# A recurrent mixer kernel on one core: the scan put last in each step of TensorE's program

## The reference, cut to what matters

```python
proj = xn @ in_proj_w.T                      # gate 8192, x 8192, B and C 8 x 128 each, dt 128
xBC  = silu(causal_conv4(xBC))               # per channel, 4 taps
# per head (128 heads of 64 channels, 8 groups of 16 heads), chunks of 128 tokens:
scores = (C @ B.T) * exp(cs[l] - cs[s]) * (s <= l)
y = scores @ (x * dt) + state terms + x * D
yg = y * silu(gate);  per group: yg * rsqrt(mean(yg**2) + eps) * norm_w
out = x_in + (yg @ out_proj_w.T) * silu(experts(xn))
```

## Time and profile before

| | |
|---|---|
| median of 3 runs | 1605.9 us (1604.34 to 1606.1) |
| profiled execution | 1605.15 us, span 1603.2 us |
| TensorE, matmul | 1588.8 us busy, 99% |
| TensorE, weight load | 1267.1 us, 79% |
| VectorE | 1409.1 us, 88% |
| ScalarE | 1196.3 us, 75% |
| GpSimd | 961.7 us, 60% |
| granted TensorE clock | 0.999 |
| a stream load, issue to landing | 2.7 us (median of 387) |
| a load of exponents | 4.3 us (median of 128) |
| one transpose, mean | 272 ns |

### The profile page before, as it was taken

One profiled execution on the slowest core, in us unless ns is written; L12 is line 12 of the kernel. 1 busy time (PEld: TensorE's weight loads), 2 busy tenths in 40 slices (PEclk: granted clock), 3 DMA queues, 4 the chain that ended last, 5 costly groups with the idle time before them and its releaser, 6 DMA issues.

```text
span 1603.2 us, 28456 instructions
## 1 busy us (share of the span) xinstructions
PE 1588.8 (99%) x8478; PEld 1267.1 (79%) x8478; DVE 1409.1 (88%) x1654; ACT 1196.3 (75%) x2305; POOL 961.7 (60%) x596
## 2 busy tenths in 40 slices
PE   9999999999999999999999999999999999999998
PEld 6888777887778777887778777887778777877776
DVE  7727899889999899889998899889998899889987
ACT  4525878777787878777787878777787878778772
POOL 6523456655666556655666556655666666656563
PEclk9999999999999999999999999999999999999999
DMA  5234344334443344344443334334443334334442
GB/s 187 75 136 148 126 137 169 118 131 143 146 140 118 127 129 169 121 129 143 148 140 118 127 129 170 121 127 144 145 139 122 127 128 163 129 122 149 151 133 85
DMA packets 83831, 216.88 MB, mean 135 GB/s; under 512 B 10576, under 2 KB 12880, under 8 KB 83536
## 3 DMA queue, kind: packets, MB, share of 16 engines
q1 hardware_dynamic: 83376, 214.55, 39.7%
q10 hardware_dynamic: 288, 0.30, 0.1%
HBM read 209.83 MB, written 4.98 MB: 134 GB/s over the span
## 4 chain that ended last, share of the span: by engine, by line
PE 84%; DVE 8%; ACT 3%; issue 3%; POOL 1%; DMA 0%; SPq 0%; ACTq 0%; DVEq 0%; POOLq 0%
PE pj L454 15%; PE pj L456 14%; PE pj L455 14%; PE pr L454 9%; PE pr L455 7%; PE pr L456 7%; PE sc L699 7%; PE sc L703 3%; PE tb L688 3%; DVE conv L1375 3%; ACT decay L967 1%; DVE wo_lo L1439 1%; DVE xc L1389 1%; PE tb L712 1%; DVE decay L1403 1%
## 5 line engine op out<-in xcount | busy, mean ns | idle before, releaser
L1079 POOL TENSOR_TENSOR w_lo<-stg,w_hi 128x512 fp32r<-128x512 f32 x316 | 496.6, 1572 | 314.5 <-ACT w_hi L941 253.0
L454 PE MATMUL pj<-xT_hi,w_hi 128*128 128x512 f32 x1208 | 476.3, 394 | 4.4 <-DVE conv L1375 1.5
L456 PE MATMUL pj<-xT_hi,w_lo 128*128 128x512 f32 x1208 | 470.8, 390 | 0.0
L455 PE MATMUL pj<-xT_lo,w_hi 128*128 128x512 f32 x1208 | 470.4, 389 | 0.0
L1375 DVE SCALAR_TENSOR_TENSOR conv<-pj,par,conv 128x510 f32<-128x510 f32 (+2 forms) x480 | 357.8, 745 | 76.2 <-ACT conv L949 63.0
L967 ACT ACTIVATE decay<-decay,dtg 128x256 f32<-128x256 f32 (+1 forms) x1024 | 378.9, 442 | 0.0
L1116 POOL TENSOR_TENSOR xc<-xc,thg 128x512 f32<-128x512 f32 x128 | 203.2, 1587 | 188.2 <-DVE xc L1426 187.6
L1122 POOL TENSOR_TENSOR sqsum<-sqsum,sq 128x512 f32<-128x512 f32 x112 | 216.8, 1936 | 115.4 <-ACT sq L995 112.2
L454 PEld LDWEIGHTS pj<-xT_hi,w_hi 128*128 128x128 f32 x1208 | 226.8, 188 | 59.7 <-issue 9.4
L456 PEld LDWEIGHTS pj<-xT_hi,w_lo 128*128 128x128 f32 x1208 | 226.8, 188 | 48.0
L455 PEld LDWEIGHTS pj<-xT_lo,w_hi 128*128 128x128 f32 x1208 | 226.9, 188 | 45.3
(11 more groups left out here) (182 smaller groups left out, 1976.5 us busy)
## 6 DMA issues: line engine op xcount, KB each, us to landing
stg<-wstream SPq DMA_DIRECT2D x387, 256.0 KB, 2.7
decay<-cs_scr SPq DMA_DIRECT2D x128, 768.0 KB, 4.3
acc<-hid SPq DMA_DIRECT2D x8, 256.0 KB, 5.2
out<-acc SPq DMA_DIRECT2D x8, 256.0 KB, 2.0
dt_scr<-decay SPq DMA_DIRECT2D x1, 1024.0 KB, 6.4
gate_scr<-part SPq DMA_DIRECT2D x4, 256.0 KB, 2.0
dtg<-dt_scr SPq DMA_DIRECT2D x16, 64.0 KB, 4.0
stg<-hid SPq DMA_DIRECT2D x4, 256.0 KB, 4.7
```

The lines of the kernel that those rows point to most:

```text
L454: nc.tensor.matmul(dst, hi_w, hi_x, start=first, stop=False)
L455: nc.tensor.matmul(dst, hi_w, lo_x, start=False, stop=False)
L456: return nc.tensor.matmul(dst, lo_w, hi_x, start=False, stop=last)
L1079: nc.gpsimd.tensor_tensor(w_dest(n, 1), stg[:, s % RING, :], f32(w_dest(n, 0)), ALU.subtract).then_inc(S["wl"], 1)
```

## The change

In each step of TensorE's program the scan moves behind the second x block and behind the part of the output projection. The other engines' programs stay as they are.

```diff
                 if has_pair(g, half, s + 1):
                     x_turn(*pair(g, half, s + 1))
-                if has_pair(g, half, s):
-                    scan(g, half, s)
                 if len(mine) > 1:
                     channel_block(g, half, mine[1])
                 if with_out:
                     out_of_step(g, half, s)
+                if has_pair(g, half, s):
+                    scan(g, half, s)
```

## The result

The changed kernel takes 1651.4 us (median of 4 runs, 1650.82 to 1651.92) against 1606.0 us (4 runs, 1604.34 to 1606.51): a ratio of 1.0282, with a 95% interval of 1.0269 to 1.0294. The prediction said 1649. The profiled execution has a span of 1649.5 us, 46.3 more than before.

What follows compares the result with a forecast made beforehand. TensorE, busy for all of a 180.5 us group, was taken as the bound, with VectorE close behind. Six half 0's at 5.3, 4.6, 2.3 and seven half 1's at 0.7 gave 43.6 us, so 1649 us; range 1617 to 1678.

Steps and rivals of the forecast that it cites:

- TensorE alone costs nothing: All moved scans: no instruction added, first scan row stays at 0.58 us, changed neighbours costed at 0.
- the 14 of the rival: Rival: each of 120 scans pays a dearer drain behind a 512-column matmul, 14 us on top, 1663 us; chance 0.05.
- One-block steps are cheap: Six of eight steps per half: scan result 2.73 + about 0.1 later; VectorE 0.95 us late at `gate_silu(4)` in half 0.
- the 1.06 us put down for x1's wait: Step 4 of half 0: block x1 waits 1.06 us for the PSUM bank that a late `gate_silu(4)` frees.
- The wait at `add_scan` and the lag behind it: VectorE's new waits of 15.8 us per group at `add_scan`; behind step 4 of half 0, 3.4 late at `gate_silu(5)`.
- Step 6 of half 0 at 3.4 us: x4 comes up 1.45 us earlier against a `gate_silu(6)` 3.4 late; TensorE loses 3.4 us there.
- Half 1 at 0.7 us: Half 1: 0.5 us at the B/C product in step 4 plus an estimated 0.2 for x2 and x5.
- The two half 0's outside the loop: First half-group costs 2.3 us; the seventh group's half 0, without the round of the loop, 4.6.
- the one by which only the lost cover costs (1622): Rival: lag made up in step 5; step 6 costs 1.45 plus 0.35, with 0.5 around it; 1622 us; chance 0.16.
- The one by which half 1 doesn't come level (1664): Rival: VectorE carries its lag from half 1 into the next half 0; group costs about 8, 1664 us; chance 0.22.
- no loss: Rival: the new wait at `add_scan` falls into VectorE's 16.6 us of idle time per group; 1605 or 1600 us; chance 0.06.
- VectorE as the bound: Rival: all 15.8 us of waits go on the path in each of 7.3 groups; 1720 us; chance 0.03.

Runs made afterwards that it cites:

- their own kernel: Kernel before with the scan moved only in the six one-block steps of each half, steps 4 and 6 left as they were: 1610.8 us, ratio 1.0027.
- the kernel with the round in half 1: Changed kernel with TensorE's loop going round at step 5 of half 1: 1672.1 us; the kernel before with the same move: 1617.3 us.
- a bad cut: Kernel before, order kept, with TensorE's loop going round right behind scan(4) of half 0, ahead of the second x block: 1648.4 us, ratio 1.0268.

## Why the prediction was right, step by step

- **TensorE alone costs nothing**: right, or nearly. The scan's first row stays at 0.58 and the number of instructions is the same. A step without any wait takes 10.30 us from gate block to gate block where it took 10.27, so over its 120 steps 3 to 4 us at most, and not the 14 of the rival. The rule of the Trainium skill (TensorEngine Tiling (Array Packing), Key Properties) that a change of tiling mode drains the array has no price in that first row that differs between the two orders.
- **One-block steps are cheap**: right. They cost 4.5 us in all by their own kernel. The 0.5 us for the output row's split is 0.38 in five of the six groups of the loop (step 1 of half 1 took 11.61 us and 11.23 before); the lag at `gate_silu(4)` was nearly gone by the time it was reached, and the 1.06 us put down for x1's wait were 0.46.
- **The wait at `add_scan` and the lag behind it**: right. 114.4 us over 7.5 groups are 15.3 per group, where 15.8 was worked out; in the two-block steps 2.6 to 3.6 each. The lag at `gate_silu(5)` was 2.7 us where 3.4 was put, and 2.2 in the kernel with the round in half 1, where gate block 5 is in time. The pause ahead of L941, which the prediction held to be ScalarE's own at its loop's round, is that: in four of the six rounds L941 begins before gate block 5 is through, and the pause stays at 2.1 to 3.3 us.
- **Step 6 of half 0 at 3.4 us**: right in its mechanism, wrong in its place. In the changed kernel x4 waits 1.3 and 2.0 us in two groups and hardly in the others. TensorE loses the rest at the round of its loop, in a pause (2.3 to 2.75 us, against 0 to 0.53) and often a fall of the clock, which the prediction didn't have: it had no term for the code load of TensorE's own loop, though it had seen ScalarE's. The kernel with the round elsewhere shows the wait where it was put, at 2.6 to 2.9.
- **Half 1 at 0.7 us**: too small. Step 5 grew by 0.89 and step 7 by 0.48, 1.4 in the group that was read (12.48 us against 11.59, and 10.75 against 10.27, each from gate block to gate block). The prediction had named new waits of TensorE in half 1 as well as in half 0 as a sign that it is wrong. They are there, 1.4 of the 6.8 us, though its own sum had put 0.7 there.
- **The sum**: 6.8 us per group where 6.0 was forecast. That the total came within 2.4 us owes something to errors that cancel: 0.6 too much for x1, 0.7 too little for half 1, and at the end of the lag a round and a clock that were not in the sum. The two half 0's outside the loop cost about 1.6 and 2.5 us, not 2.3 and 4.6, which takes back some of what the groups in the loop cost over the forecast. That part is luck. Of the rivals, the one by which only the lost cover costs (1622) describes the kernel with the scan between block and output part (1619.9), not this one. The one by which half 1 doesn't come level (1664) fell: `gate_silu(4)` of half 0 begins 5.56 us behind its gate block (950.37 against 944.81) where it was 5.42. So did dearer drains, no loss, and VectorE as the bound.

What stays open: how the 45.4 us divide between the lag and the exposed round; each alone brings a large part, and they overlap. A round's pause goes with its code packet: where the packet begins 2.1 to 3.2 us before the end of the work ahead of it, the pause is 0 to 0.54 us, at 0.7 to 2.0 us it is 0.6 to 1.8, within half a microsecond of that end 2.1 to 2.75, and 1.7 to 2.9 us after it 4.3 to 5.5. Why the packet begins when it does isn't shown; that the engine gets less far ahead over a short scan is argued.

## What to carry to other kernels

When an instruction is moved later on the engine that sets the time, nothing is lost there; look for the in-order queue that reads its result, see what stands behind that reader, and follow this work back to the first engine. A wait of 3 us in a queue with no pauses behind it comes back in full, be it at another place than the one you name. A pause on the bound engine isn't a cost of its own until a kernel without it is faster: two kernels that only moved it were slower, because the lag was still there, and with the lag gone taking it away gave some 11 us. Look too at where an edit leaves the end of a loop's body: a short group just ahead of it covers less of the code load.

## What the runs showed of the hardware

- A round of TensorE's loop showed idle time from 0 to 5.5 us, by where the body was cut, with the same instructions in the same order; in the kernel before a bad cut costs 42 us of 1606. At each of 75 rounds a 16 KB packet of code landed 1.5 to 1.9 us before the first row behind the round.
- After pauses of 2.3 to 2.75 us the granted clock was 0.50 (1.2 GHz) for some 3.4 us in four of six cases, and stayed at 1.00 in two: a 512-column matmul then takes 0.43 us from start to start instead of 0.23.
- VectorE's `x_silu` takes 0.68 us where no instruction of GpSimd is running as it begins (51 of 52 in the kernel before), and 1.12 us or more, mostly 1.78, where one is (108), so that moving one engine's work by a microsecond changes another's durations.
